# Attention in a perceiver block: four transposed pairs weighted per visit, a minimum per chunk, and narrow products for the inverse sums

## The reference, cut to what matters

```python
x = x + cross_attention(layernorm(x), ctx, bias)     # x (4,128,512), ctx (4,2048,512), bias (128,2048)
x = x + hgrn_block(layernorm(x))                     # ternary projections, a recurrence over 128 tokens
x = x + moe(layernorm(x))                            # 8 experts, top 2

# cross_attention, 16 heads of 32:
logits  = einsum('bhqd,bhkd->bhqk', q, k) + bias
weights = softmax(logits, axis=-1)
x       = einsum('bhqk,bhkd->bhqd', weights, v)
```

## Time and profile before

| | |
|---|---|
| median of three runs | 1007.76 us |
| profiled execution, its own time | 1008.51 us |
| its span on the core | 1006.7 us |
| TensorE (PE) busy | 972.1 us, 97% |
| VectorE (DVE) busy | 610.7 us, 61% |
| ScalarE (ACT) busy | 488.5 us, 49% |
| bias additions, first chunk of a head (L712) | 64 x 685 ns |
| bias additions, later chunks | 192 x 751 ns |
| exponentials (L894) | 64 x 2010 ns |
| transposes of pairs (L502) | 1024 records, 274 ns |
| products with v (L517) | 2048 records, 276 ns |
| granted TensorE clock, mean | 0.996 |

### The profile page before, as it was taken

The page is one execution under the profiler, slowest core; times in us unless marked ns, Lnnn a source line. Parts: engine busy times, 40 slices in busy tenths (PEclk is TensorE's granted clock), DMA queues, the critical chain, the costliest instruction groups (busy, mean ns, idle before and its releaser), DMA issues. The chain is left out here.

```text
span 1006.7 us, 18245 instructions
## 1 busy us (share of the span) xinstructions
PE 972.1 (97%) x7342; PEld 816.5 (81%) x7350; DVE 610.7 (61%) x1193; ACT 488.5 (49%) x633; POOL 263.0 (26%) x258
## 2 busy tenths in 40 slices
PE   9999999999999999999999999977899999999996
PEld 7888788888788888788888787654589999999995
DVE  6517895556895567886454885787852112455552
ACT  3211885171886055786151787578621102455551
POOL 2203830002830001840000850688400101111100
PEclk9999999999999999999999999999999999999998
DMA  8294861524761615771431778300079949699930
GB/s 292 71 190 86 178 151 48 209 88 122 176 163 49 274 42 177 173 188 49 160 101 42 176 161 298 125 1 1 33 266 380 373 157 341 218 381 351 345 100 13
DMA packets 77596, 169.92 MB, mean 169 GB/s; under 512 B 6472, under 2 KB 17608, under 8 KB 72384
## 3 DMA queue, kind: packets, MB, share of 16 engines
q1 hardware_dynamic: 75392, 163.87, 53.1%
q0 software_dynamic: 2112, 4.80, 2.0%
HBM read 119.01 MB, written 16.10 MB: 134 GB/s over the span
## 5 line engine op out<-in xcount | busy, mean ns | idle before, releaser
L995 POOL CAST stack<-kT 128x2048 fp32r<-128x2048 f32 x32 | 62.9, 1981 | 381.3 <-ACT kT L850 373.9
L712 DVE CUSTOM_DVE_ANT_0 prob<-psum,biasmap,top 128x512 f32<-128x512 f32 x192 | 144.2, 751 | 15.5 <-PE psum L482 7.0
L894 ACT ACTIVATE prob<-prob,top 128x2048 f32<-128x2048 f32 x64 | 128.6, 2010 | 37.7 <-DVE top L712 37.7
L2352 PE MATMUL psum<-xT,wring 128*128 128x128 f32 (+3 forms) x1024 | 134.0, 291 | 0.4 <-ACT xT L2706 0.4
L502 PE MATMUL psum<-ident,prob 128*128 128x128 f32 x1024 | 130.8, 274 | 1.3 <-ACT probT L902 1.3
L2352 PEld LDWEIGHTS psum<-xT,wring 128*128 128x128 f32 x1024 | 130.4, 191 | 1.8 <-ACT xT L2706 0.7
L502 PEld LDWEIGHTS psum<-ident,prob 128*128 128x128 f32 x1024 | 116.7, 140 | 16.0 <-issue 4.4
L850 ACT COPY kT<-psum 128x512 f32<-128x512 f32 x64 | 37.3, 585 | 189.1 <-PE psum L414 189.0
L429 PE MATMUL psum<-wv_hi,ctx_part 128*128 128x512 f32 x256 | 99.9, 390 | 0.1
L431 PE MATMUL psum<-wv_hi,ctx_part 128*128 128x512 f32 x256 | 99.6, 389 | 0.0
L430 PE MATMUL psum<-wv_lo,ctx_part 128*128 128x512 f32 x256 | 99.6, 389 | 0.0
(11 more groups left out here) (285 smaller groups left out, 1789.8 us busy)
## 6 DMA issues: line engine op xcount, KB each, us to landing
wring<-in_w SPq DMA_DIRECT2D x64, 1024.0 KB, 8.5
ctx_raw<-in_ctx_t SPq DMA_DIRECT2D x15, 1024.0 KB, 6.2
stack<-stack SPq DMA_DIRECT2D x32, 256.0 KB, 4.7
early_stack<-early_stack SPq DMA_DIRECT2D x28, 256.0 KB, 4.0
prob<-in_w_gate_t SPq DMA_DIRECT2D x1, 5632.0 KB, 17.1
stack<-key_stack SPq DMA_DIRECT2D x20, 256.0 KB, 4.0
query_stacks<-prob SPq DMA_DIRECT2D x16, 256.0 KB, 5.4
qstack<-query_stacks SPq DMA_DIRECT2D x16, 256.0 KB, 5.2
```

What stands on the lines that cost most here:

```text
L712: dve.tensor_tensor_reduce(prob[:, slot, keys], psum[:, scores.of[n, j, c], :], biasmap[:, keys], 1.0, top[:, h, (c + 1) % 2:(c + 1) % 2 + ...
L894: act.activation(prob[:, slot, :], prob[:, slot, :], ACT.Exp, bias=top[:, h, 1:2], scale=-1.0, accum_out=top[:, h, 2:3]).then_inc(*raised. ...
L2352: mm = pe.matmul(psum[:, w, 0:width], wring[piece][:, k, h % 4 * P:(h % 4 + 1) * P], xT[:, q % 2, k, 0:width], start=(k == 0), stop=(k == ...
```

## The change

Three things. `TOGETHER` becomes 4: outside `TAIL`, a visit follows steps 5, 9, 13, 17 and 21 only (slots 7, 3, 7, 3, 7) and multiplies the four pairs t-5 to t-2; in `TAIL` it stays two. The places of the copied pairs are laid out anew, so what a copy waits for changes. Each chunk writes a minimum of its own, with no wait on the chunk before, and `find_least` takes the minimum of the four: that of head j-1 is issued after the first bias addition of head j, that of head 3 after the quad's last one. `spread_sums` loses its spreading copy and becomes `invert_sums`; `turn_sums` becomes four products of 32 output rows that read a column of `rinv` 32 times against the identity, and it stands after slot 7.

```diff
-TOGETHER = 2
+TOGETHER = 4
-SUMS_AT = 5
+SUMS_AT = 7
...
-        top = sb("top", [P, HEADS, 3], F32, region_r)
+        top = sb("top", [P, 2 * QUAD, UNITS + 2], F32, region_r)
...
         def weighed_behind(t):
-            if t % TOGETHER < TOGETHER - 1 or t < TOGETHER + WEIGH_LATER - 1:
-                return ()
-            return range(t - WEIGH_LATER - TOGETHER + 1, t - WEIGH_LATER + 1)
+            if t not in TAIL:
+                return range(t - TOGETHER - 1, t - 1) if t % TOGETHER == 1 and t > TOGETHER else ()
+            return range(t - 3, t - 1) if t % 2 else ()
...
         def turned_pair(n, p):
             first = prob_slot(n, 0)
-            if p // TOGETHER % 2 == 0:
...
+            if p in (0, 1, 5, 6):
+                return probT[:, p % 5 if p < 6 else 1, :].rearrange("p (i j q) -> p i j q", i=2, j=QUAD)
+            if p == LAST:
+                return prob[:, first + QUAD - 1, HALF:].rearrange("p (i j q) -> p i j q", i=2, j=QUAD)
+            head, lo = first + (0 if p == 2 else 2), CHUNK if p == TOGETHER else 0
+            return prob[:, head:head + 2, lo:lo + CHUNK].rearrange("p i (j q) -> p i j q", j=QUAD)
 
         def turned_place_free(n, p):
...
+            if p < 2:
+                return multiplied.at(n - 1, p + 5) if n else None
+            return multiplied.at(n, p - 5) if p in (5, 6) else None
...
             def turn_sums(n):
...
-                pe.transpose(psum[:, w, 0:P], inverse[:, :], ident[:, :]).then_inc(*sums_turned.made(n))
+                for j in range(QUAD):
+                    mm = pe.matmul(psum[j * DH:(j + 1) * DH, w, 0:P], rinv[:, n % 2, j:j + 1].broadcast_to([P, DH]),
+                                   ident[:, :], start=True, stop=True, tile_position=(0, j * DH))
+                mm.then_inc(*sums_turned.made(n))
...
-                elif g >= 2 and (j, c) == (QUAD - 1, 0):
+                elif g >= 2 and (j, c) == (2, 0):
                     dve.wait_ge(*multiplied.at(n - 2, LAST))
-                if c:
-                    dve.wait_ge(*biased.at(n, j, c - 1))
                 dve.wait_ge(*scored.at(n, j, c))
                 dve.tensor_tensor_reduce(
-                    prob[:, slot, keys], psum[:, scores.of[n, j, c], :], biasmap[:, keys], 1.0,
-                    top[:, h, (c + 1) % 2:(c + 1) % 2 + 1] if c else HIGHEST, ALU.add, ALU.min,
-                    top[:, h, c % 2:c % 2 + 1]).then_inc(*biased.made(n, j, c))
+                    prob[:, slot, keys], psum[:, scores.of[n, j, c], :], biasmap[:, keys], 1.0, HIGHEST, ALU.add,
+                    ALU.min, top[:, slot, c:c + 1]).then_inc(*biased.made(n, j, c))
+
+            def find_least(n, j):
+                slot = prob_slot(n, j)
+                dve.wait_ge(*biased.at(n, j, UNITS - 1))
+                dve.tensor_reduce(top[:, slot, UNITS:UNITS + 1], top[:, slot, 0:UNITS], AX.X,
+                                  ALU.min).then_inc(*biased.made(n, j, "least"))
...
                         for c in (2 * half, 2 * half + 1):
                             add_bias(n, j, c)
+                            if j and c == 0:
+                                find_least(n, j - 1)
+                        if i == SLOTS_OF_QUAD - 1:
+                            find_least(n, j)
...
             def raise_head(n, j):
-                act.wait_ge(*biased.at(n, j, UNITS - 1))
+                act.wait_ge(*biased.at(n, j, "least"))
```

More of the change, by code:

```diff
@@ L287, in perceiver_block, with chunks_and_least @@
         keys_low_g = events("keys_low_g", [n for n in quads if n % DT])
-        scored, biased = (events(name, [(n, j, c) for n in quads for j in range(QUAD) for c in range(UNITS)])
-                          for name in ("scored", "biased"))
+        def chunks_and_least(n, j):
+            before = [(n, j - 1, "least")] if j else []
+            after = [(n, j, "least")] if j == QUAD - 1 else []
+            return [(n, j, 0), *before, *((n, j, c) for c in range(1, UNITS)), *after]
+        scored = events("scored", [(n, j, c) for n in quads for j in range(QUAD) for c in range(UNITS)])
+        biased = events("biased", [key for n in quads for j in range(QUAD) for key in chunks_and_least(n, j)])
         raised = events("raised", [(n, j) for n in quads for j in range(QUAD)])
@@ L298, in perceiver_block @@
         moved_a = events("moved_a", [(n, p) for n, p in pairs if not by_vector(n, p)])
-        spread_out = events("spread_out", quads)
+        sums_inverted = events("sums_inverted", quads)
         sums_turned, sums_copied = events("sums_turned", quads), events("sums_copied", quads)
@@ L356, in turned_pair @@
             first = prob_slot(n, 0)
-            if p // TOGETHER % 2 == 0:
[L358 to L363, removed]
-        def turned_place_free(n, p):
[L367 to L371, removed]
+            if p in (0, 1, 5, 6):
[4 more added lines that the diff above has]
+            return prob[:, head:head + 2, lo:lo + CHUNK].rearrange("p i (j q) -> p i j q", j=QUAD)
+        def turned_place_free(n, p):
+            if p < 2:
+                return multiplied.at(n - 1, p + 5) if n else None
+            return multiplied.at(n, p - 5) if p in (5, 6) else None
         def raw_piece(b, p):
@@ L524, in turn_sums @@
                            (2, scores.hold(2, ("sums", n), sums_copied.at(n))))
-                pe.wait_ge(*spread_out.at(n))
+                pe.wait_ge(*sums_inverted.at(n))
                 pe.wait_ge(*free)
-                pe.transpose(psum[:, w, 0:P], inverse[:, :], ident[:, :]).then_inc(*sums_turned.made(n))
+                for j in range(QUAD):
+                    mm = pe.matmul(psum[j * DH:(j + 1) * DH, w, 0:P], rinv[:, n % 2, j:j + 1].broadcast_to([P, DH]),
+                                   ident[:, :], start=True, stop=True, tile_position=(0, j * DH))
+                mm.then_inc(*sums_turned.made(n))
             def turn_and_weigh(b, t):
@@ L695, in add_bias @@
                 b, g = divmod(n, DT)
-                h, slot = QUAD * g + j, prob_slot(n, j)
+                slot = prob_slot(n, j)
                 keys = slice(c * CHUNK, (c + 1) * CHUNK)
@@ L723, in move_pair, with invert_sums, copy_sums @@
                     "p i (j q) -> p i j q", j=QUAD)).then_inc(*moved_v.made(n, p))
-            def spread_sums(n):
-                g = n % DT
+            def invert_sums(n):
                 dve.wait_ge(*raised.at(n, QUAD - 1))
-                dve.reciprocal(rinv[:, n % 2, :], top[:, QUAD * g:QUAD * (g + 1), 2]).then_inc(*own.made())
-                dve.wait_ge(*own.last())
+                first = prob_slot(n, 0)
+                dve.reciprocal(rinv[:, n % 2, :], top[:, first:first + QUAD, UNITS + 1]).then_inc(*sums_inverted.made(n))
+            def copy_sums(n):
+                dve.wait_ge(*sums_turned.at(n))
                 if n >= 1:
                     dve.wait_ge(*weighted.at(n - 1))
[L732 to L737, removed]
                 dve.tensor_copy(inverse[:, :], psum[:, scores.of["sums", n], 0:P]).then_inc(*sums_copied.made(n))
@@ L827, in vector_attention @@
                         if i == 3 and n > DT * b:
-                            spread_sums(n - 1)
+                            invert_sums(n - 1)
                         if i == SUMS_AT and n > DT * b:
@@ L836, in vector_attention @@
                 finish(last - 1)
-                spread_sums(last)
+                invert_sums(last)
                 split_chunk(CHUNKS * (b + 1))
@@ L841, in vector_attention @@
                 finish(last)
-            return move_pair, spread_sums, copy_sums, finish, add_attention
+            return move_pair, invert_sums, copy_sums, finish, add_attention
         def scalar_attention(act):
@@ L891, in raise_head @@
             def raise_head(n, j):
-                h, slot = QUAD * (n % DT) + j, prob_slot(n, j)
-                act.wait_ge(*biased.at(n, j, UNITS - 1))
-                act.activation(prob[:, slot, :], prob[:, slot, :], ACT.Exp, bias=top[:, h, 1:2], scale=-1.0,
-                               accum_out=top[:, h, 2:3]).then_inc(*raised.made(n, j))
+                slot = prob_slot(n, j)
+                act.wait_ge(*biased.at(n, j, "least"))
+                act.activation(prob[:, slot, :], prob[:, slot, :], ACT.Exp, bias=top[:, slot, UNITS:UNITS + 1],
+                               scale=-1.0, accum_out=top[:, slot, UNITS + 1:UNITS + 2]).then_inc(*raised.made(n, j))
             def move_pair(n, p):
@@ L1488, in tensor_recurrence, with vector_recurrence @@
             route(3)
-        def vector_recurrence(dve, move_pair, spread_sums, copy_sums, finish, add_attention):
+        def vector_recurrence(dve, move_pair, invert_sums, copy_sums, finish, add_attention):
             own = vector_own
```

## The result

The changed kernel takes 1024.59 us, the median of four runs (1024.25 to 1025.75), against 1007.43 for the kernel before beside it: a ratio of 1.0158, 95% interval 1.0138 to 1.0178. It is slower by 17 us. 1026 was forecast.

A forecast was written before the change was run, and what follows sets the result against it. TensorE, busy 97% of the span, was taken as the bound, with what it waits for. Quads 1 to 3 add 1.0, 1.5 and 2.0 us: 4.5 a batch, 18 for four, plus 0.3, giving 1026 us; 8-in-10 range 1007 to 1032.

The forecast's parts named there:

- Both waits: TensorE in quads 2 and 3: slot 6's transposes idle about 1.2 us for ScalarE's copy, slot 3's second score chunk about 1 for VectorE.
- the half quad behind it: TensorE from slot 6's transposes to the next quad's first scores: 4.48 us, where it took 3.62 before.
- S_4 to S_4: Sign in TensorE's timeline: from slot 4's scores to the next quad's slot 4 scores, 17.7 us instead of 16.3.
- a chunk 0.61: VectorE's bias additions: a later chunk holds it 0.61 us instead of 0.80, twelve per quad giving 2.3 us.
- Where the least is found. This is what I think decides.: Slots 4 to 7: exponential 1 waits for the late least, delaying slot 6's transposes; +0.83 us in each of quads 1 to 3.
- Places: Pair 0's copy waits for pair 5's product in slot 3's visit: costs nothing; up to 0.5 us per quad if ScalarE were early.
- the removed visits count: Rival: exponential 1 gets its least in time, TensorE saves 5.6 us of visits and pays 2.7 for sums; 992 to 1005, chance 0.14.
- only the late exponential: Rival: VectorE's gain clears slot 3's scores, only slot 6's transposes wait; +1.3 us a batch, about 1013 us, chance 0.17.
- pair 6 in slot 0 of quad 3: Quad 3, slots 0 to 3: VectorE moves pair 6 as well as pair 7, delaying slot 4's scores; +1.15 us.
- Quad 1: First exponential waits for its chunk and least, later copies follow late; quad 2 starts at 124.25 instead of 123.23: +1.0 us.
- Quad 2: +0.65 us in slots 0 to 3 (VectorE's pair 7 copy) and +0.83 in the other half (late exponential 1).
- The sums: Four inverse-sum products behind a visit instead of one transpose: +0.15 us per quad, +2.4 over 16; bounds 0 and 0.83.

The follow-up runs named there:

- visits_only: Kernel before with four pairs per visit and the new places, but its chained minimum and old sums by one transpose: 1025.37 us, ratio 1.0169.
- minimum_only: Kernel before with a minimum per chunk and find_least where the change has it, two-pair visits and old sums: 1008.69 us, ratio 1.0004.
- least_at_once: Changed kernel with each head's least found right behind its own fourth chunk instead of behind the next head's first: 1021.49 us, ratio 1.0136.
- places: Changed kernel with copied pairs laid out so that no copy waits for a product, the least still late: 1023.74 us, ratio 1.0142.
- places_once: Changed kernel with places that no copy waits for and the least found right behind its head's own chunks: 1020.75 us, ratio 1.0108.
- pair7_scalar: Changed kernel with pair 7 of quads 0 and 1 copied by ScalarE instead of VectorE: 1014.65 us, ratio 1.0055.
- sums_only: Kernel before with the inverse sums by four narrow products after slot 5 and no spreading copy: 1007.57 us, ratio 0.9989.

## Why the prediction was right or wrong

**Right: the time, the sign, where TensorE idles.** Both waits were named with slot and engine, and came out as reckoned: T_6 4.50 after S_4 (4.50), the half quad behind it 4.47 (4.48), S_3's second chunk 4.13 after S_1 (4.1 to 4.2), S_4 to S_4 17.63 (17.7), a chunk 0.61. A least is 0.15 long, but holds VectorE for only 0.07. VectorE's rows around slot 4 of quad 2:

```profile
134.18 0.69 DVE L715 CUSTOM_DVE_ANT_0 prob<-psum,biasmap 128x512 f32<-128x512 f32 x1
134.80 0.08 DVE L715 DVE_READ_ACCUMULATOR2_ANT top<- 128x1 f32 x1
134.80 0.15 DVE L722 TENSOR_REDUCE top<-top 128x1 f32<-128x4 f32 x1
134.87 0.68 DVE L715 CUSTOM_DVE_ANT_0 prob<-psum,biasmap 128x512 f32<-128x512 f32 x1
```

**Wrong: "Where the least is found. This is what I think decides."** By itself it does not. The late least is one of two waits ahead of exp 1, and each suffices. The step that failed is "Places", priced at nothing because ScalarE "gets there about then". I had both times in hand, exp 0's end and M_3's pair 5, and did not follow them through two copies of 0.95 to exp 1: that gives 1.24 after S_4, 0.2 short of the late least. Two waits of nearly one length; I named the longer one as the cause. T_6's time came out because the wait that I had left out happened to end those 0.2 earlier, and that is luck. The visits and places lose all 17 us without a late least (visits_only), the late least with two-pair visits nothing on balance (minimum_only), removing either wait from the change little (least_at_once 3 us, places 1), and removing both 4 to 5, with a third wait in their place (places_once).

So my rival "the removed visits count" also had the wrong point from which it decides. An exp 1 with its least by S_4 + 0.3 could not have started then: ScalarE was not free. The rival "only the late exponential" failed where the prediction had doubted it: S_3 did wait, and VectorE's copy of pair 7 is what it waited for (pair7_scalar).

**Wrong: a pair in the wrong slot.** I let VectorE copy pair 6 in slot 0 of quad 3 and made that +1.15. In that slot stands pair 6 of quad 1, which ScalarE copies; pair 6 of quad 2, the one that VectorE has, comes in the tail. Measured +0.52, like quad 2's 0.55. It is 2.5 us of my 18.

**The other terms.** Quad 1 +0.82 (+1.0). Quad 2 +0.55 +0.83 (+0.65 +0.83). The sums 0.25 more (0.15 taken), hidden in the kernel before (sums_only) and paid behind M_7, where M_7 is shorter than reckoned by about as much (1.77 for 1.92). The forecast was 18.3, the slots and tails measured 14.7. The total came closer than that by luck: in the profile 1.7 us outside the attention was added, which nothing in my sum stood for and which may be scatter.

**The two rules.** That a change of tiling mode drains TensorE (the Trainium skill, "TensorEngine Tiling (Array Packing)", section Key Properties) held for TensorE's own work: 0.97 from T_7 to M_7 after (139.44 to 140.41), as before, and 0.3 a quad saved. It says nothing of waits, and in quad 2 these grew by 1.7. The factor of four for float32 transposes (the Trainium skill, "TensorE: Matmul & The Clock Gate", section Terms) does not hold here: the sums' four products are 8 records in 0.40 us, two groups, a factor of two over the one transpose.

## What to carry to other kernels

Work that is packed into fewer, longer visits leaves gaps where it stood. Before it is moved, check each such gap: does the helper's chain (here a 2.0 us exponential and a 1.0 us copy for every 2.7 us of scores and transposes) still fit it? A visit full of products costs nothing only while it hides a chain of its own length.

Two waits that end together hide each other: undoing one showed 3 us, the other 1, and both 4 to 5, because a third came up behind them. Undoing the part that caused them gave 14, but that takes in the separate wait of S_3 too, for which one edit gave 10 (pair7_scalar). Test a cause by adding it alone to the old kernel as well as by removing it from the new one, and follow an in-order helper through all that it does, not only the instruction that changed.
